# A graph layer on one core: edges over 128 partitions instead of 125, ScalarE with four of the step rows in three groups, and one copy of v moved

## The chip, the cores and the metric

The kernel runs on one core of a Trainium2 chip. The metric is the device time in microseconds (us) of one execution. The program is a single launch.

## The reference

625 nodes with 256 features each, 20,000 edges (`src`, `dst`) sorted by `dst`, and one layer of three parts. What is computed:

```
xn  = layernorm(x)
gnn = (segment_sum(xn[src], dst) / max(count(dst), 1)) @ W_l.T + xn @ W_r.T + b_r
q, k, v = split(xn @ Wqkv.T + bqkv)            # 8 heads of 32
y   = 0.5*(qn.kn)^2 v + sqrt(32)*(qn.kn) v + 32*sum(v), divided by the same with v = 1
x   = x + gnn + y @ Wproj.T + bproj
x   = x + ffn(layernorm(x))                    # GELU, 8 experts, each token takes its best
```

The part that the change touches is the neighbour sum. It isn't gathered row by row: the kernel builds the matrix A (how many edges lead from node s to node t) and multiplies it with `xn @ W_l.T` later.

## The kernel before, in words

**Tiles of nodes.** `TP = 125` nodes make a tile, there are `T = 5` of them, and activations lie as 125 partitions x 5 tiles.

**The matrix A from one-hot products.** The 20,000 edges lie over 125 partitions in 160 chunks (one column of `edges_sb` is a chunk). `GC = 5` chunks make a group, `NG = 32` groups make 16 pairs. For every chunk two rows of 628 half-precision numbers per partition are written into the tensor `oh` (in `mem`): a node row (`node_ids == dst`, always by VectorE, L728) and a step row (whether the column is past `src`). The step rows of a group are shared out by `act_steps(g)`: the first three are ScalarE's (a Sign activation in `step_rows`, L523) and the other two VectorE's (L731). TensorE then accumulates, per chunk, (node row, cut to one tile of 128 columns) times (step row), as two matmuls, L1010 (501 columns) and L1012 (126 columns), in `products(g, tile)`. It accumulates cumulative counts; their differences give A.

**Which tile.** Since edges are sorted by `dst`, a group mostly lies in one tile of nodes. ScalarE, TensorE, VectorE and GpSimd work out in the first 18 us which tile it is and whether there is a second one (`ge`, `edge_tiles`, `flags`). `pair(p)` multiplies two groups for their first tiles, and behind a branch (`other_tiles`) again for a second tile. With the given inputs the five tiles have 3984, 4055, 3973, 4034 and 3954 edges; groups of 625 edges that have two tiles are 6, 12, 19 and 25, which gives (32 + 4) x 5 = 180 calls of the two matmuls.

**Ring of buffers.** `oh` has `OHB = 7` groups; a group g from 7 on may be written when `oh_free` says that group g - 7 (and the pair it is in) was multiplied. VectorE announces a group by `oh_ready`, ScalarE by `steps_ready`; TensorE waits for both before each group.

**Order written out by hand.** All engines have a fixed program. Between the pairs TensorE does 14 small jobs in PSUM bank 7, which are chained by `b7_full` (TensorE to reader) and `b7_free` (reader to TensorE):

- `sums()` (L1044), read by VectorE into `MA` and `ks` (L782, L783). VectorE does groups 3 to 6 before it and 7 and 8 behind it.
- five transposes of q and k (L1051), copied by ScalarE (L598). ScalarE does groups 8 and 9 before the first copy.
- four products U (L1069), read by VectorE into `uq` (L792). VectorE does this before groups 19, 21, 23 and 25.
- four products N (L1074) of `uq`, copied by ScalarE (L606). They stand before pairs (24,25), (26,27), (28,29) and (30,31). Their copies stand on ScalarE behind groups 26, 28, 30 and 31. N number j + 1 waits for `b7_free` of copy j.

When the last pair is done, seven tiny matmuls (L1077) announce `A_done`. ScalarE, VectorE and GpSimd wait for it, then come the differences, attention (L1096, L1117), the projection, the gated network and the experts.

**ScalarE ahead of the pairs** (L549 to L593): the Sign activations of the first groups lie between the copies of the transposed x (`xT_copy`), the squares of q and k (`square`, which wait for VectorE's `biased`), two square roots, and five copies of v and z out of PSUM (`vz_copy`, L572). TensorE clears the banks of A when the copies are made: banks 4, 5, 6 after three copies, bank 0 after four (L999 to L1003), and then starts pair 0. The projection into these banks does not wait for the copies.

Of the kernel before, what the change touches and what calls it, by code (L numbers as in the profile page):

```python
# [6 lines left out]
F16 = mybir.dt.float16  # L7
BF16 = mybir.dt.bfloat16
I32 = mybir.dt.int32
U32 = mybir.dt.uint32  # L10
ALU = mybir.AluOpType
# [3 lines left out]
P = 128  # L15
# [4 lines left out]
def gps_layer(nc, x, edges, w_qkv, b_qk, b_v, w_lr, b_r, w_proj, b_proj, temp,  # L20
              w1, b1, wg, bg, wd, bd, rows_sorted, out):
    N, C = out.shape
    TP = 125
    T = N // TP
    KC = C // P
    NCH = edges.shape[2]
    GC = 5
    NG = NCH // GC
    NP = NG // 2
    OHB = 7  # L30
    OHW = TP * (T - 1) + P
# [14 lines left out]
    assert EB <= T  # L46
    assert N == T * TP and NG * GC == NCH and H == 2 * HG

    with ExitStack() as ctx:
        def sb(name, shape, dt=F32):  # L50
            return ctx.enter_context(nc.sbuf_tensor(name, shape, dt))

        def sem(name):
            return ctx.enter_context(nc.semaphore(name))
# [5 lines left out]
        x_all = sb("x_all", [P, T, C])  # L60
        x_sb = x_all[0:TP]
        edges_sb = sb("edges_sb", [P, 2, NCH], I32)
        src_i, dst_i = edges_sb[0:TP, 0], edges_sb[0:TP, 1]
        wqkv_sb = sb("wqkv_sb", [P, KC, 3 * C])
        bqk_all = sb("bqk_all", [P, 2 * C])
        bqk_sb = bqk_all[0:TP]
# [14 lines left out]
        WD = E * KH * C  # L81
        OH = OHB * 2 * GC * OHW // 2
        BIG = 2 * KH * N
        assert OH + 6 * N <= WD + BIG and T * (N + 1) <= WD
        mem = sb("mem", [P, WD + BIG])
# [1 line left out]
        big = mem[:, WD:WD + BIG]  # L87
        ident = sb("ident", [P, P])
        blk = sb("blk", [P, P])
        node_ids = sb("node_ids", [TP, OHW], F16)  # L90
        ids_m1 = sb("ids_m1", [TP, OHW], F16)
        ones_c = sb("ones_c", [P, P])
        sc2_col = sb("sc2_col", [P, 1])
        root = sb("root", [P, 1])
        base_col = sb("base_col", [P, 1])
        zeros = sb("zeros", [TP, BANK], BF16)
        thr = sb("thr", [TP, T + 1])
        below = sb("below", [TP, T - 1])
        erank = sb("erank", [TP, E])

        src_f = sb("src_f", [TP, NCH])
        dst_f = sb("dst_f", [TP, NCH])
        half_src = sb("half_src", [TP, NCH])
        tile_of = sb("tile_of", [1, T, NG])
        edge_tiles = sb("edge_tiles", [1, 2, T - 1, NG])
        between = sb("between", [1, T, NG])
        span = sb("span", [1, NG])
        two_code = sb("two_code", [1, NG])
        more_code = sb("more_code", [1, NG])
        ones_col = sb("ones_col", [TP, 1], BF16)  # L110
        pair_hi = sb("pair_hi", [1, NP])
        flags = sb("flags", [1, NP], I32)
        more = sb("more", [1, T, NG], I32)
        at_sb = sb("at_sb", [P, T * N])
        QB = P + 1
        qk_sb = sb("qk_sb", [P, T * 4 * QB])
        oh = mem[0:TP, 0:OH].bitcast(BF16).rearrange("p (b w j n) -> p b w j n", b=OHB, w=2, j=GC)
        cum = mem[0:TP, 0:T * (N + 1)].rearrange("p (t n) -> p t n", t=T)
        ge = at_sb[0:TP, 2 * T * C:2 * T * C + (T - 1) * NCH // 2].bitcast(BF16).rearrange("p (k g j) -> p k g j", k=T - 1, j=GC)
        hT = big[:, 0:KH * N].rearrange("p (k n) -> p k n", k=KH)  # L120
        hT_step = big[:, KH * N:KH * N + EB * KH * TP].rearrange("p (b k n) -> p b k n", b=EB, k=KH)

# [41 lines left out]
        PW = N + N % 2  # L164
        lgT = yT_sb[:, 0:N]
        perm = at_sb[0:TP, 0:T * PW // 2].bitcast(BF16).rearrange("p (t n) -> p t n", t=T)
# [18 lines left out]
        pos_f = sb("pos_f", [TP, T])  # L185
# [39 lines left out]
        steps_ready = sem("steps_ready")  # L225
# [34 lines left out]
        flag_read = sem("flag_read")  # L260
# [62 lines left out]
            yield AT[:, 4, TW:N], ps[0:TP, 6, 0:TP]  # L323


        def act_steps(g):
            return 3


        QKV_BANKS = (7, 4, 5, 6, 0, 4, 5, 6, 0, 7)  # L330
# [20 lines left out]
        def x_bank(j):  # L351
            return ps[:, 4 + j, :]
# [162 lines left out]
        def _(act):  # L515
# [5 lines left out]
            def step_rows(g, first, last):  # L521
                for j in range(first, last):
                    ins = nc.scalar.activation(oh[:, g % OHB, 0, j, :], ids_m1[:, :], ACT.Sign,  # L523
                                               bias=half_src[:, g * GC + j:g * GC + j + 1])
                return ins

            def fill(g):
                if g >= OHB:
                    act.wait_ge(oh_free, g - OHB + 1)
                step_rows(g, 0, act_steps(g)).then_inc(steps_ready, 1)  # L530
# [5 lines left out]
            def square(t):  # L536
                act.wait_ge(qk_ready, t + 1)
                nc.scalar.activation(sq[:, t, :].rearrange("p (b c) -> p b c", b=4), qk[:, t, :, 0:P], ACT.Square
                                     ).then_inc(sq_ready, 1)
# [8 lines left out]
            def xT_copy(j):  # L548
                own = slice(2 * TP * j, min(2 * TP * (j + 1), N))  # L549
                act.wait_ge(xT_ps, j + 1)  # L550
                nc.scalar.copy(xnT[:, :, own], x_bank(j)[:, 0:KC * (own.stop - own.start)].rearrange(  # L551
                    "p (c n) -> p c n", c=KC)).then_inc(xT_copied, 1)
# [9 lines left out]
            xT_copy(0)  # L562
            root_part(1)
            step_rows(0, 2, act_steps(0)).then_inc(steps_ready, 1)
            fill(1)
            xT_copy(1)
            square(0)
            xT_copy(2)

            def vz_copy(t):  # L570
                act.wait_ge(qkv_ps, T + t + 1)
                nc.scalar.copy(vz[:, t, 0:2 * C], ps[0:TP, QKV_BANKS[T + t], :]).then_inc(vz_ready, 1)  # L572

            square(1)
            fill(2)
            step_rows(3, 0, 1)
            square(2)
            square(3)
# [4 lines left out]
            nc.scalar.activation(nrm[:, :, 0, :], nrm[:, :, 0, :], ACT.Sqrt, scale=SC2)  # L583
            nc.scalar.activation(nrm[:, :, 1, :], nrm[:, :, 1, :], ACT.Sqrt).then_inc(std_ready, 1)
            step_rows(3, 2, act_steps(3)).then_inc(steps_ready, 1)
            vz_copy(1)
            vz_copy(2)
            fill(4)
            vz_copy(3)
            fill(5)  # L590
            vz_copy(4)
# [23 lines left out]
            for u, (hg, hf, m, pr) in enumerate(units):  # L615
                lo, hi = HALF[hf]
                w = hi - lo
# [3 lines left out]
                b = 2 * (u % SLOTS)  # L621
# [52 lines left out]
        def _(dve):  # L674
# [24 lines left out]
            def normalised(n):  # L699
                lo, hi = LN_PARTS[n]  # L700
                dve.wait_ge(std_ready, n + 1)
                step(nc.vector.reciprocal(rstd[:, lo:hi], rstd[:, lo:hi]))
                for t in range(lo, hi):
                    nc.vector.tensor_scalar(xn[:, t, :], x_sb[:, t, :], mv[:, t, 0:1], rstd[:, t:t + 1],
                                            ALU.subtract, ALU.mult).then_inc(xn_ready, 1)
# [9 lines left out]
            variances(2, T)  # L715
            dve.wait_ge(flag_sum, 1)
            past_first = ps[0:1, 0, 0:(T - 1) * NG].rearrange("p (k g) -> p k g", k=T - 1)
            nc.vector.tensor_scalar(edge_tiles[:, 0], past_first, GC * TP - 1.0, None, ALU.is_gt)
            nc.vector.tensor_scalar(edge_tiles[:, 1], past_first, 1.0 - GC * TP, None, ALU.is_gt).then_inc(flag_read, 1)
            normalised(1)  # L720
            dve.wait_ge(ids_ready, 1)

            def fill(g):
                if g >= OHB:
                    dve.wait_ge(oh_free, g - OHB + 1)
                for j in range(GC):
                    col = g * GC + j
                    ins = nc.vector.tensor_scalar(oh[:, g % OHB, 1, j, :], node_ids[:, :], dst_f[:, col:col + 1], None,  # L728
                                                  ALU.is_equal)
                    if j >= act_steps(g):  # L730
                        ins = nc.vector.tensor_scalar(oh[:, g % OHB, 0, j, :], ids_m1[:, :], src_f[:, col:col + 1], 2.0,  # L731
                                                      ALU.is_ge, ALU.mult)
                ins.then_inc(oh_ready, 1)

            def fill_past(job):
                for g in dve_groups(job):
                    fill(g)
# [6 lines left out]
            def head_sums(t):  # L744
                dve.wait_ge(sq_ready, t + 1)
                return nc.vector.tensor_reduce(nrm[:, t].rearrange("p w h -> p (w h)"),
                                               sq[:, t, :].rearrange("p (h d) -> p h d", d=D), AX.X, ALU.add)

            fill(0)
            dve.wait_ge(in_bqk, 16)  # L750
            biased(0)
            biased(1)
            head_sums(0)
            fill(1)
            biased(2)
            head_sums(1)
# [77 lines left out]
            for t in range(T):  # L834
                a, rest = (ps[0:TP, b, :] for b in RP_BANKS[t % 2])
# [56 lines left out]
            step(nc.vector.tensor_reduce(pos_f[:, :], at_e[:, :, :].rearrange("p e t -> p t e"), AX.X, ALU.add))  # L892
            nc.vector.tensor_copy(pos[:, :], pos_f[:, :]).then_inc(pos_ready, 1)  # L893
            for t in range(T):
                nc.vector.tensor_scalar(perm[:, t, :], node_ids[:, 0:PW], pos_f[:, t:t + 1], None, ALU.is_equal
                                        ).then_inc(perm_ready, 1)

            step(nc.vector.tensor_tensor(past[:, :, :], ahead[0:1, 1:E, 0:1].broadcast_to([1, E - 1, T - 1]),
# [43 lines left out]
        def _(pe):  # L942
# [62 lines left out]

            def products(g, tile):
                buf = g % OHB
                for j in range(GC):
                    node_of = oh[:, buf, 1, j, bass.ds(tile * TP, P)]
                    mm(psf[:, bass.ds(tile * BANK, TW + 1)], node_of, oh[:, buf, 0, j, 0:TW + 1],  # L1010
                       start=False, stop=False, skip_group_check=True)
                    mm(psf[:, bass.ds(tile * P + 5 * BANK, AW)], node_of, oh[:, buf, 0, j, TW:N + 1],  # L1012
                       start=False, stop=False, skip_group_check=True)
# [145 lines left out]
            for t in range(T):  # L1159
# [3 lines left out]
                b, b2 = RP_BANKS[t % 2]  # L1163
# [39 lines left out]
            for part in range(2):  # L1203
                lo, hi = columns(part)
                for k in range(KH):
                    n = KH * part + k
# [72 lines left out]


_OUT = (625, 256)


# [42 lines left out]
```

## Time and profile before

| | us |
|---|---|
| median of 3 runs | 252.06 |
| lowest, highest | 251.73, 252.9 |
| the profiled execution's own time | 251.73 |
| its span, first to last instruction | 250.0 |
| TensorE busy | 235.7 (94%) |
| VectorE busy | 148.2 (59%) |
| ScalarE busy | 145.2 (58%) |
| GpSimd busy | 31.7 (13%) |
| mean granted TensorE clock | 0.997 of full speed |

A busy share is a mean over the span. The one-hot stage lies from about 11 us to 92.6 us; in it VectorE and ScalarE are nearly always busy, and after it much less. What bounds a stretch is read from the chain of work that ended last and from the timelines of the engines beside it.

### The profile page before, as it was taken

How to read it: one execution, taken by the hardware profiler on the slowest of the kernel's cores; microseconds unless marked ns; L12 is line 12 of the kernel's file. 1: busy time of each engine (PE TensorE's matmuls, PEld its weight loads, DVE VectorE, ACT ScalarE, POOL GpSimd, SP SyncE). 2: the span in 40 equal slices, each digit the busy share in tenths (PEclk: the TensorE clock that was granted, in tenths of full speed). 3: DMA queues.
4: the chain of work that ended last, by engine and by line, in shares of the span. 5: the costliest groups of instructions: out<-in, count | busy, mean ns of one | idle time of the engine just before them, and what ended most of it. 6: DMA issues, size and time to landing. Idle time of an engine off the chain costs nothing.

```text
span 250.0 us, 4726 instructions
## 1 busy us (share of the span) xinstructions
PE 235.7 (94%) x1428; PEld 149.4 (60%) x1429; DVE 148.2 (59%) x422; ACT 145.2 (58%) x223; POOL 31.7 (13%) x64
## 2 busy tenths in 40 slices
PE   7899999999897999999999999998899999999990
PEld 2448676655454553433378886564455578888880
DVE  2999999999999969950134649523700243223320
ACT  3977998999999967899950116443043332333000
POOL 7460000000000019100000000000540000000331
PEclk9999999999999999999999999999999999999998
DMA  6560000000000000199910000030123000000111
GB/s 233 194 215 3 1 3 5 3 4 5 0 5 3 3 3 3 37 413 425 416 59 4 0 0 0 24 134 9 32 79 106 0 1 3 0 1 3 38 34 33
DMA packets 6030, 15.82 MB, mean 63 GB/s; under 512 B 2724, under 2 KB 3783, under 8 KB 4723
## 3 DMA queue, kind: packets, MB, share of 16 engines
q1 hardware_dynamic: 4432, 12.64, 13.6%
q0 software_dynamic: 1280, 1.31, 2.0%
q10 hardware_dynamic: 288, 1.44, 1.4%
q8 instruction: 21, 0.34, 0.6%
q14 instruction: 9, 0.07, 0.1%
HBM read 14.08 MB, written 1.30 MB: 62 GB/s over the span
## 4 chain that ended last, share of the span: by engine, by line
PE 69%; DVE 26%; ACT 1%; issue 1%; POOL 1%; DVEq 0%; POOLq 0%
PE ps L1276 17%; DVE mem L728 14%; PE ps L1214 7%; PE ps L1096 7%; PE ps L1260 6%; DVE mem L731 6%; PE ps L1117 5%; PE ps L1176 4%; PE ps L1010 4%; PE ps L1244 3%; PE ps L945 3%; PE ps L1165 2%; PE ps L1167 2%; PE ps L973 1%; DVE qk_sb L774 1%
## 5 line engine op out<-in xcount | busy, mean ns | idle before, releaser
L523 ACT ACTIVATE mem<-ids_m,half_src 125x628 bf16<-125x628 f16 x96 | 69.8, 815 | 0.0
L1010 PE MATMUL ps<-mem 125*128 125x501 bf16 x180 | 51.3, 374 | 2.2 <-issue 2.0
L728 DVE TENSOR_SCALAR mem<-node_ids,dst_f 125x628 bf16<-125x628 f16 x160 | 52.1, 371 | 0.0
L1276 PE MATMUL ps<-mem 128*125 x192 | 41.6, 379 | 0.0
L1012 PE MATMUL ps<-mem 125*128 125x126 bf16 x180 | 39.3, 219 | 0.0
L1276 PEld LDWEIGHTS ps<-mem 128*125 128x125 f32 x192 | 36.0, 188 | 5.4
L1010 PEld LDWEIGHTS ps<-mem 125*128 x180 | 17.6, 98 | 22.5 <-issue 4.8
L622 ACT ACTIVATE qk_sb<-ps,sc_col 125x626 f32<-125x626 f32 (+1 forms) x40 | 28.6, 779 | 3.7 <-PE ps L1096 3.7
L731 DVE TENSOR_SCALAR mem<-ids_m,src_f 125x628 bf16<-125x628 f16 x64 | 23.9, 374 | 0.0
L671 ACT COPY mem<-mem 128x1000 f32 x8 | 8.2, 1031 | 19.8 <-PE ps L1276 19.8
L1096 PE MATMUL ps<-mem 32*125 32x313 f32 (+1 forms) x160 | 19.1, 472 | 0.2 <-DVE mem L801 0.2
L1012 PEld LDWEIGHTS ps<-mem 125*128 x180 | 17.5, 97 | 2.3 <-issue 1.2
L1214 PE MATMUL ps<-xnT,w_sb 128*128 128x375 f32 (+1 forms) x64 | 18.4, 432 | 0.0
L935 DVE SCALAR_TENSOR_TENSOR row<-vz,row x12 | 5.8, 485 | 20.1 <-issue 20.1
L920 DVE COPY mem<-mem 128x500 f32 (+2 forms) x12 | 4.1, 393 | 20.3 <-ACT mem L663 20.0
L505 POOL DMA_INDIRECT rows_sorted<-row,pos x5 | 6.2, 1236 | 77.3 <-DVE pos L893 76.1
L1260 PE MATMUL ps<-xnT,w_sb 128*128 128x512 f32 (+1 forms) x56 | 15.3, 433 | 0.0
L1117 PE MATMUL ps<-qk_sb,vz 125*32 125x313 f32 (+1 forms) x160 | 14.7, 439 | 0.6 <-ACT qk_sb L622 0.6
L1096 PEld LDWEIGHTS ps<-mem 32*125 32x125 f32 x160 | 8.9, 180 | 10.5 <-issue 5.0
L1214 PEld LDWEIGHTS ps<-xnT,w_sb 128*128 128x128 f32 x64 | 11.6, 189 | 5.5 <-ACT mem L651 1.2
L973 PE MATMUL ps<-wqkv_sb,xnT 128*125 128x512 f32 (+1 forms) x40 | 14.1, 487 | 0.8 <-ACT xnT L551 0.8
L651 ACT ACTIVATE mem<-ps,b_sb 128x375 f32<-128x375 f32 (+1 forms) x16 | 8.3, 522 | 9.4 <-PE ps L1214 9.4
(204 smaller groups left out, 280.0 us busy)
## 6 DMA issues: line engine op xcount, KB each, us to landing
mem<-in_wd SPq DMA_DIRECT2D x8, 1024.0 KB, 13.1
w_sb<-in_w SPq DMA_DIRECT2D x1, 1024.0 KB, 8.2
vz<-in_bd SPq DMA_DIRECT2D x1, 1000.0 KB
wqkv_sb<-in_w_qkv ACTq DMA_DIRECT2D x1, 768.0 KB, 6.1
x_all<-in_x ACTq DMA_DIRECT2D x1, 640.0 KB, 4.7
row<-rows_sorted SPq DMA_DIRECT2D x1, 579.7 KB
wlr_sb<-in_w_lr SPq DMA_DIRECT2D x1, 512.0 KB, 5.5
bqk_all<-in_b_qk SPq DMA_DIRECT2D x1, 256.0 KB, 4.7
```

What stands on the lines that cost most here:

```text
L523: ins = nc.scalar.activation(oh[:, g % OHB, 0, j, :], ids_m1[:, :], ACT.Sign, bias=half_src[:, g * GC + j:g * GC + j + 1])
L622: nc.scalar.activation(gsq[:, u % NGB, :, 0:w], ps[0:TP, b:b + 2, 0:w], ACT.Square, bias=sc2_col[0:TP, :]).then_inc(g_ready, 1)
L728: ins = nc.vector.tensor_scalar(oh[:, g % OHB, 1, j, :], node_ids[:, :], dst_f[:, col:col + 1], None, ALU.is_equal)
L731: ins = nc.vector.tensor_scalar(oh[:, g % OHB, 0, j, :], ids_m1[:, :], src_f[:, col:col + 1], 2.0, ALU.is_ge, ALU.mult)
L973: ins = mm(ps[0:TP, QKV_BANKS[n], lo:hi], xnT[:, c, TP * t:TP * (t + 1)], w[:, c, :], start=(c == 0), stop=(c == KC - 1))
L1010: mm(psf[:, bass.ds(tile * BANK, TW + 1)], node_of, oh[:, buf, 0, j, 0:TW + 1], start=False, stop=False, skip_group_check=True)
L1012: mm(psf[:, bass.ds(tile * P + 5 * BANK, AW)], node_of, oh[:, buf, 0, j, TW:N + 1], start=False, stop=False, skip_group_check=True)
L1096: ins = mm(ps[0:TP, 2 * ((2 * u2 + h // 2) % SLOTS) + h % 2, 0:hi - lo], kT[rows, hg, TP * m:TP * (m + 1)], qT[rows, hg, lo:hi], start=Tru ...
L1117: ins = mm(ps[D * h:D * (h + 1), 6 + k % 2, 0:hi - lo], v[:, m, P * hg + D * h:P * hg + D * (h + 1)], gsq[:, (2 * u2 + pr) % NGB, i, 0:hi ...
L1214: ins = mm(fa_bank(part, k), w1_sb[:, c, P * k:P * (k + 1)], x2nT[:, c, lo:hi], start=(c == 0), stop=(c == KC - 1))
L1260: ins = mm(psf[:, at + lo:at + hi], w1_sb[:, c, P * k:P * (k + 1)], x2nT[:, c, lo:hi], start=(c == 0), stop=(c == KC - 1))
L1276: ins = mm(ps[0:TP, 4 + n % EB, 0:C], hT_step[:, n % EB, k, :], wd_sb[:, bass.ds(e, 1), k, :], start=(k == 0), stop=(k == KH - 1))
```

## The change

`edges` is laid out on the host as 160 chunks of 128 edges: 20,000 real edges fill 156 chunks and 32 places of chunk 157; spare places have `src = 0` and `dst = 627`, a column that no tile's output uses. Tensors that were `[TP, ...]` on this path become `[P, ...]` with P = 128 partitions, and the thresholds that tell tiles apart count `GC * P`. Group 31 has two chunks to multiply instead of five (`chunks(g)`). Groups 2, 3 and 9 have four step rows by ScalarE and one by VectorE; of group 31's two, one each. One row of group 2 is written earlier on ScalarE, and `vz_copy(2)` stands behind group 4 instead of ahead of it.

```diff
+    CHUNKS = -(-_EDGES // P)
-        src_i, dst_i = edges_sb[0:TP, 0], edges_sb[0:TP, 1]
+        src_i, dst_i = edges_sb[:, 0], edges_sb[:, 1]
-        node_ids = sb("node_ids", [TP, OHW], F16)
-        ids_m1 = sb("ids_m1", [TP, OHW], F16)
+        node_ids = sb("node_ids", [P, OHW], F16)
+        ids_m1 = sb("ids_m1", [P, OHW], F16)
...
-        oh = mem[0:TP, 0:OH].bitcast(BF16).rearrange(...)
+        oh = mem[:, 0:OH].bitcast(BF16).rearrange(...)
...
+        def chunks(g):
+            return min(GC, CHUNKS - g * GC)
+
         def act_steps(g):
-            return 3
+            if g in (2, 3, 9):
+                return 4
+            return 3 if chunks(g) == GC else chunks(g) // 2
...
             xT_copy(1)
+            step_rows(2, 0, 1)
             square(0)
             xT_copy(2)
...
             square(1)
-            fill(2)
+            step_rows(2, 1, act_steps(2)).then_inc(steps_ready, 1)
             step_rows(3, 0, 1)
...
             step_rows(3, 2, act_steps(3)).then_inc(steps_ready, 1)
             vz_copy(1)
+            fill(4)
             vz_copy(2)
-            fill(4)
             vz_copy(3)
...
-            nc.vector.tensor_scalar(edge_tiles[:, 0], past_first, GC * TP - 1.0, None, ALU.is_gt)
+            nc.vector.tensor_scalar(edge_tiles[:, 0], past_first, GC * P - 1.0, None, ALU.is_gt)
...
@@ fill(g) of VectorE @@
-                for j in range(GC):
+                for j in range(chunks(g)):
@@ products(g, tile) of TensorE @@
-                for j in range(GC):
+                for j in range(chunks(g)):
...
+    def chunked(numbers, fill):
+        spare = np.full(160 * 128 - _EDGES, fill, numbers.dtype)
+        return np.concatenate([numbers, spare]).reshape(160, 128).T
...
-        "edges": partitions(np.stack([a[k].reshape(-1, tp).T for k in ("src", "dst")], axis=1)),
+        "edges": np.ascontiguousarray(np.stack([chunked(a["src"], 0), chunked(a["dst"], 627)], axis=1)),
```

## Rows read from the trace of the kernel before

**Rows 1.** The chain that ended last: start us, us, what held it.

```profile
36.72 0.29 DVE mem L731
37.01 0.20 DVE MA L782
...
75.77 0.46 DVE yT_sb L792
76.27 0.80 PE ps L1074 x2
...
90.96 0.06 issue
91.02 0.37 PE ps L1010
...
92.75 0.69 DVE mem L801
```

**Rows 2.** Busy time by stretch, 28.7 to 92.7 us; us, then busy of PE, PEld, DVE, ACT, POOL.

```profile
28.70:36.90 8.20, 8.20 (x66) 5.78 (x65) 8.20 (x29) 8.20 (x13) 0.00 (x0) 1.00 0.01 3
36.90:39.90 3.00, 3.00 (x25) 1.87 (x23) 3.00 (x14) 2.05 (x4) 0.00 (x0) 1.00 0.02 5
39.90:57.10 17.20, 16.84 (x129) 10.28 (x128) 17.20 (x60) 17.20 (x26) 0.00 (x0) 1.00 0.01 3
57.10:76.20 19.10, 17.17 (x116) 9.54 (x113) 19.10 (x65) 19.10 (x28) 0.00 (x0) 1.00 0.01 3
76.20:92.70 16.50, 15.54 (x110) 8.82 (x111) 14.35 (x50) 14.61 (x23) 0.00 (x0) 1.00 0.01 3
```

**Rows 3.** VectorE in order of time, 28 to 98 us: start, us, instruction.

```profile
28.73 1.25 DVE L728 TENSOR_SCALAR mem<-node_ids,dst_f 125x628 bf16<-125x628 f16 x4
...
30.78 1.25 DVE L728 TENSOR_SCALAR mem<-node_ids,dst_f 125x628 bf16<-125x628 f16 x4
...
36.93 0.28 DVE L782 TENSOR_TENSOR MA<-ps,blk 128x128 f32<-128x128 f32 x1
...
90.18 0.38 DVE L731 TENSOR_SCALAR mem<-ids_m,src_f 125x628 bf16<-125x628 f16 x1
```

**Rows 4.** TensorE in order of time, 24 to 58 us.

```profile
27.88 1.03 PE L945 MATMUL ps<-zeros 125*128 125x512 bf16 x4
28.74 0.38 PE L1010 MATMUL ps<-mem 125*128 125x501 bf16 x1
...
34.20 2.48 PE L1044 MATMUL ps<-qk_sb 125*128 125x129 f32 x20
36.51 0.38 PE L1010 MATMUL ps<-mem 125*128 125x501 bf16 x1
...
39.24 0.62 PE L1051 MATMUL ps<-ident,qk_sb 125*128 125x125 f32 x4
```

**Rows 5.** TensorE in order of time, 88 to 93 us.

```profile
88.83 0.77 PE L1074 MATMUL ps<-yT_sb,blk 128*128 128x312 f32 x2
...
90.53 0.37 PE L1010 MATMUL ps<-mem 125*128 125x501 bf16 x1
...
91.02 0.37 PE L1010 MATMUL ps<-mem 125*128 125x501 bf16 x1
91.29 0.38 PE L1010 MATMUL ps<-mem 125*128 125x501 bf16 x1
...
92.38 0.16 PE L1038 MATMUL ps<-zeros 125*128 125x2 bf16 x1
92.40 0.31 PE L1077 MATMUL ps<-zeros 125*128 125x2 bf16 x7
```

**Rows 6.** ScalarE in order of time, 12 to 41 us; brackets: idle before.

```profile
12.63 0.56 ACT L551 COPY xnT<-ps 128x500 f32<-128x500 f32 x1
14.03 0.63 ACT L538 ACTIVATE at_sb<-qk_sb 125x512 f32<-125x512 f32 x1 [0.84 <-DVE qk_sb L741]
...
24.62 0.59 ACT L572 COPY vz<-ps 125x512 f32<-125x512 f32 x1 [0.54 <-PE ps L973]
25.11 2.24 ACT L523 ACTIVATE mem<-ids_m,half_src 125x628 bf16<-125x628 f16 x3
27.25 0.57 ACT L572 COPY vz<-ps 125x512 f32<-125x512 f32 x1
...
39.90 0.58 ACT L598 COPY mem<-ps 128x500 f32<-128x500 f32 x1 [0.95 <-PE ps L1051]
```

**Rows 7.** ScalarE in order of time, 87 to 92 us.

```profile
87.75 0.52 ACT L606 ACTIVATE mem<-ps,base_col 128x313 f32<-128x313 f32 x1
88.16 2.25 ACT L523 ACTIVATE mem<-ids_m,half_src 125x628 bf16<-125x628 f16 x3
90.28 0.52 ACT L606 ACTIVATE mem<-ps,base_col 128x312 f32<-128x312 f32 x1
```

More of the change, by code:

```diff
@@ L97, in gps_layer @@
         thr = sb("thr", [TP, T + 1])
-        below = sb("below", [TP, T - 1])
+        below = sb("below", [P, T - 1])
         erank = sb("erank", [TP, E])
-        src_f = sb("src_f", [TP, NCH])
-        dst_f = sb("dst_f", [TP, NCH])
-        half_src = sb("half_src", [TP, NCH])
+        src_f = sb("src_f", [P, NCH])
+        dst_f = sb("dst_f", [P, NCH])
+        half_src = sb("half_src", [P, NCH])
         tile_of = sb("tile_of", [1, T, NG])
@@ L109, in gps_layer @@
         more_code = sb("more_code", [1, NG])
-        ones_col = sb("ones_col", [TP, 1], BF16)
+        ones_col = sb("ones_col", [P, 1], BF16)
         pair_hi = sb("pair_hi", [1, NP])
@@ L116, in gps_layer @@
         qk_sb = sb("qk_sb", [P, T * 4 * QB])
-        oh = mem[0:TP, 0:OH].bitcast(BF16).rearrange("p (b w j n) -> p b w j n", b=OHB, w=2, j=GC)
+        oh = mem[:, 0:OH].bitcast(BF16).rearrange("p (b w j n) -> p b w j n", b=OHB, w=2, j=GC)
         cum = mem[0:TP, 0:T * (N + 1)].rearrange("p (t n) -> p t n", t=T)
-        ge = at_sb[0:TP, 2 * T * C:2 * T * C + (T - 1) * NCH // 2].bitcast(BF16).rearrange("p (k g j) -> p k g j", k=T - 1, j=GC)
+        ge = at_sb[:, 2 * T * C:2 * T * C + (T - 1) * NCH // 2].bitcast(BF16).rearrange("p (k g j) -> p k g j", k=T - 1, j=GC)
         hT = big[:, 0:KH * N].rearrange("p (k n) -> p k n", k=KH)
@@ L717, in _ @@
             past_first = ps[0:1, 0, 0:(T - 1) * NG].rearrange("p (k g) -> p k g", k=T - 1)
-            nc.vector.tensor_scalar(edge_tiles[:, 0], past_first, GC * TP - 1.0, None, ALU.is_gt)
-            nc.vector.tensor_scalar(edge_tiles[:, 1], past_first, 1.0 - GC * TP, None, ALU.is_gt).then_inc(flag_read, 1)
+            nc.vector.tensor_scalar(edge_tiles[:, 0], past_first, GC * P - 1.0, None, ALU.is_gt)
+            nc.vector.tensor_scalar(edge_tiles[:, 1], past_first, 1.0 - GC * P, None, ALU.is_gt).then_inc(flag_read, 1)
             normalised(1)
@@ L894, in _ @@
             for t in range(T):
-                nc.vector.tensor_scalar(perm[:, t, :], node_ids[:, 0:PW], pos_f[:, t:t + 1], None, ALU.is_equal
+                nc.vector.tensor_scalar(perm[:, t, :], node_ids[0:TP, 0:PW], pos_f[:, t:t + 1], None, ALU.is_equal
                                         ).then_inc(perm_ready, 1)
@@ L1281 @@
 _OUT = (625, 256)
+_EDGES = 20000
 def kernel(**inputs):
```

## Prediction, on record before the changed kernel ran

> **What bounds the kernel now.** I read the chain of work that ended last first, then the busy times by stretch, and then the timelines of the three engines side by side. The chain stands on VectorE almost without a break from about 28.8 to 76.2 us, then crosses to TensorE (the product N that waits for the last `uq`) and stays there until `A_done` at about 92.7 us [rows 1]. The busy times say the same: VectorE has no gap up to 76.2 us, TensorE has gaps of 1.93 us between 57.1 and 76.2 us, and behind 76.2 us VectorE runs out of work and TensorE sets the end [rows 2]. ScalarE has no gap either from 57.1 to 76.2 us [rows 2]: it is a near second, and the question of this change is whether it becomes the first. After `A_done` everything is released by it, and I let the rest of the kernel move as a block: no transfer or engine behind it has a start of its own that the change moves.
>
> **Prices.** VectorE makes one row (node or step) every 0.293 us: seven rows lie between the starts at 28.73 and 30.78 us, 2.05 us [rows 3]. ScalarE makes one in 0.713 us: three rows lie between the starts at 25.11 and 27.25 us, 2.14 us [rows 6]. TensorE takes 0.27 us for a chunk's two matmuls, the starts at 91.02 and 91.29 us [rows 5].
>
> The page "VectorE: DVE Perf Modes" of the Trainium skill (section "The DRAIN you can't avoid") says that a next operation does not start until the pipe is empty. By it a row would be worth its whole length, 0.37 us, and the one row that counts below would save 0.08 us more. The trace disagrees: four rows that are 1.25 us long together are part of a pace of 0.293 us each [rows 3], so I stay with the pace.
>
> **The change part by part.**
>
> *VectorE before `sums`.* Groups 2 and 3 lose a step row each on VectorE: 2 x 0.293 = 0.59 us. VectorE would reach `MA` (L782) at 36.93 - 0.59 = 36.34 us [rows 3]. But `MA` reads what TensorE's `sums()` writes, and these 20 matmuls end at 34.20 + 2.48 = 36.68 us by their row, or at 36.51 us by the start of the next one [rows 4]. TensorE doesn't get there sooner: from 27.88 us on it works through four bank clears and two pairs without a wait [rows 4]. So a new wait stands at `MA`, and most of the two rows is lost in it. Behind it are VectorE's groups 7 and 8 and all later ones, and for these TensorE. VectorE starts `MA` at about 36.72 us, 0.04 us behind the modelled end, as L801 does behind L1077 (92.75 against 92.40 + 0.31 = 92.71 us) [rows 1, 5]. Gain 0.21 us; bounds 0 (a longer wake-up than this) and 0.42 us (matmul really ends at 36.51 us). I take 0.21, since it goes by the row's own end.
>
> *VectorE, group 9.* One row less behind `MA`: 0.29 us. Bounds 0.29 and 0.37 us, the row's length. VectorE's last `uq`, which releases N 0 at 76.27 us, is then 0.21 + 0.29 = 0.50 us sooner. VectorE has no wait for a free buffer on the way (it never idles [rows 2]), and TensorE, with its 1.93 us of gaps there, can follow.
>
> *ScalarE's three extra rows* cost 3 x 0.713 = 2.14 us if nothing covers them. Group 2's lies between `xT_copy(1)` and `square(0)`, where ScalarE idles 0.84 us for VectorE [rows 6]: 0.71 us fits, cost 0; `square(0)`, `xT_copy(2)` behind it stay where they are. Group 3's pushes `vz_copy(1)` by 0.71 us. Then the moved copy counts: `vz_copy(2)` had waited 0.54 us for its projection [rows 6], and behind group 4 its data are there, so that idle time goes. By starts: `vz_copy(3)` begins at about 27.30 instead of 27.25 us and ScalarE is 0.05 us late (0.17 us at most, 0.71 - 0.54). Group 9's row comes before the first copy of transposed q and k, ahead of which ScalarE idles 0.95 us [rows 6]: 0.95 - 0.17 - 0.71 leaves at least 0.07 us. From the copy at 39.90 us on ScalarE keeps its old times. Cost 0 in all; if the covers were gone, 2.14 us, which is the slower rival.
>
> *The moved copy's other side.* TensorE clears banks 4, 5, 6 after `vz_copy(2)` and bank 0 after `vz_copy(3)`. The former now ends near 27.4 us instead of 25.2, the first clear starts at 27.88 us, and the fourth some 0.6 us later, by when `vz_copy(3)` (27.30 + 0.57 = 27.87 us) is done [rows 4, 6]. Cost 0; bounds 0 and 0.3 us. ScalarE issues no DMA here, and no queue is passed.
>
> *The last group.* VectorE has 3 rows for 7, ScalarE 1 for 3, so group 31 is ready before TensorE is. It had waited: the last chunk of group 30 starts at 90.53, one chunk later would be 90.80, and group 31 starts at 91.02 us [rows 5]. Gain 0.22 us. Three chunks fewer to multiply: 3 x 0.27 = 0.81 us, on the chain. Groups of 640 edges with two tiles are 6, 12, 18 and 25 (the tiles' edge counts end at 3984, 8039, 12012, 16046), again four, so 177 calls instead of 180; 18 and 19 are one pair, so no branch is added.
>
> *ScalarE's guard at N 3.* N 3 (88.83 us) waits for ScalarE's copy of N 2, which ends at 87.75 + 0.52 = 88.27 us and does not move [rows 5, 7]. So what arrives from VectorE is cut off at 88.83 - 88.27 = 0.56 us. The 0.50 us passes.
>
> *128 partitions instead of 125.* The trace has no row of these forms on 128 partitions. Nearest: ScalarE's copies take 0.58 us for 128x500 and 0.57 to 0.59 us for 125x512 [rows 6]. I take 0. The upper bound is 128/125, 2.4% of VectorE's 39.5 us from `MA` to 76.2 us and of TensorE's 16.3 us at the end: 0.95 + 0.39 = 1.3 us. A gain below 0 has no mechanism: no row shrinks.
>
> **Sum.** 0.21 + 0.29 + 0.22 + 0.81 = 1.53 us off `A_done`. The profiled execution took 251.73 us (span 250.0, 1.73 around it): 250.2 us. The median of the runs is 0.33 us above it, so 252.06 - 1.53 = 250.5 us.
>
> **Rivals.**
>
> *Only the tail counts (251.0 us).* The new wait at `MA` eats all of the two rows, or ScalarE is a little late at 39.90 us and its copy holds N 3 at the old time. Then 0.22 + 0.81 = 1.03 us remains. For it: the margins are thin, 0.07 us on ScalarE and 0.06 us at N 3. Against it: each would have to be missed by half a us to take the whole 0.50.
>
> *ScalarE becomes the bound (252.7 us, slower).* Place: N 3's wait for the copy of N 2. If the idle times do not take the three rows, ScalarE is 2.14 us late, the copy ends at 90.41 us, N 3 starts at about 90.47 instead of 88.83 (+1.64), and the tail gives back 1.03: +0.61 us. From 0.56 us of delay it costs, and from 1.59 us on the kernel is slower. For it: ScalarE is without a gap from 57.1 us on. Against it: the idle times of 0.84, 0.54 and 0.95 us stand where the rows are put.
>
> *128 partitions cost (251.8 us).* The upper bound above, 1.3 us, against the gain of 1.53: -0.2 us. For it nothing but the lack of a row; against it the equal copies.
>
> *The change doesn't do what it says.* The chunks do go, and 180 to 177 is sure from the inputs. It could be taken back behind `A_done`; nothing there has a fixed time, so I give it no price of its own and put it with the one above.
>
> **How the numbers follow.** The forecast has 0.69, with its own range 250.1 to 251.0; the tail alone 0.13; ScalarE the bound 0.08; 128 partitions or a gain taken back 0.10. The range for 8 in 10 takes in the tail-only case and nearly the partitions': 249.9 to 251.9 us. Half a per cent, about what a measurement tells from no change, is 1.26 us: below 250.80 us is faster. Of the forecast 0.59 lies below it and 0.10 above; the tail case is all within (0.13); of the rest 0.12 is within and 0.06 slower. Faster 0.59, same 0.35, slower 0.06.
>
> **What would show it.** Right: VectorE idle for up to 0.4 us before L782 with PE L1044 named, and the last `uq` near 75.2 us; ScalarE's gaps before L538 (0.84) and L598 (0.95) gone or under 0.2 us, the copy of N 2 still near 87.75 us; N 3 near 88.3 us; no wait before group 31; 177 calls of L1010; L801 near 91.2 us; rows on VectorE still 0.293 us apart. Wrong: N 3 waiting for ScalarE's L606, pair 0 later than 28.74 us, a wait on TensorE before a group for ScalarE's rows, or a distance between L801 and the end that differs from before's.

## The result, and the profile after

The changed kernel takes 250.26 us (median of 6 runs, 250.15 to 250.71) against 252.09 us before (6 runs, 251.68 to 252.9). The ratio is 0.9929, 95% interval 0.9914 to 0.9944. Forecast were 250.5 us, with 249.9 to 251.9 as the range. The profiled executions differ by less: 251.73 to 250.31 us, spans 250.0 to 248.6 us, 1.4 us. One of the six runs of e5_group9 took 344.03 us at a granted clock of 0.659 and is left out as a slow run; every other run here is a fast one.

Where the 1.4 us are is seen at three places of the timelines. First VectorE of the changed kernel, 20 to 98 us (start, us, instruction, in brackets the idle time before it), to be held against [rows 3]:

```profile
36.09 0.38 DVE L738 TENSOR_SCALAR mem<-ids_m,src_f 128x628 bf16<-128x628 f16 x1
36.84 0.29 DVE L789 TENSOR_TENSOR MA<-ps,blk 128x128 f32<-128x128 f32 x1 [0.37 <-PE ps L1051]
...
75.32 0.53 DVE L799 SCALAR_TENSOR_TENSOR yT_sb<-ps,ks,mem 128x312 f32<-128x312 f32 x1
...
91.34 2.63 DVE L808 COPY mem<-ps 125x501 f32<-125x501 f32 x5 [2.32 <-PE ps L1084]
```

The wait that the forecast put ahead of `MA` is there, 0.37 us, and names the matmuls of `sums` (now L1051). `MA` starts only 0.09 us sooner than before, although VectorE had two rows less to do. The last `uq` starts 0.37 us sooner (75.69 before), the copies behind `A_done` 1.41 us sooner. Then TensorE, as in [rows 4] and [rows 5]:

```profile
27.93 1.03 PE L952 MATMUL ps<-zeros 125*128 125x512 bf16 x4
...
34.33 2.48 PE L1051 MATMUL ps<-qk_sb 125*128 125x129 f32 x20
...
88.46 0.78 PE L1081 MATMUL ps<-yT_sb,blk 128*128 128x312 f32 x2
...
90.16 0.37 PE L1017 MATMUL ps<-mem 128*128 128x501 bf16 x1
90.42 0.37 PE L1017 MATMUL ps<-mem 128*128 128x501 bf16 x1
90.69 0.38 PE L1017 MATMUL ps<-mem 128*128 128x501 bf16 x1
90.97 0.17 PE L1045 MATMUL ps<-zeros 125*128 125x2 bf16 x1
90.99 0.31 PE L1084 MATMUL ps<-zeros 125*128 125x2 bf16 x7
```

Pair 0 starts at 28.79 us (before 28.74), later by just as much as the clears (27.93 against 27.88), so this is the stage's start, and not the sign against the forecast that a pair 0 held up by the moved copy would have been. N 3 starts at 88.46 instead of 88.83 us (0.37). Of the three L1017 rows at the end the first is the last chunk of group 30; group 31 follows it without a gap and has two chunks. From N 3 to L1084 it is 2.53 us, before it was 3.57: 1.04 us. And ScalarE, as in [rows 6] and [rows 7]:

```profile
13.14 0.82 ACT L529 ACTIVATE mem<-ids_m,half_src 128x628 bf16<-128x628 f16 x1
14.08 0.63 ACT L544 ACTIVATE at_sb<-qk_sb 125x512 f32<-125x512 f32 x1
...
24.27 0.56 ACT L579 COPY vz<-ps 125x512 f32<-125x512 f32 x1
24.73 2.24 ACT L529 ACTIVATE mem<-ids_m,half_src 128x628 bf16<-128x628 f16 x3
26.87 1.05 ACT L579 COPY vz<-ps 125x512 f32<-125x512 f32 x2
...
40.03 0.58 ACT L605 COPY mem<-ps 128x500 f32<-128x500 f32 x1 [0.28 <-PE ps L1058]
...
87.88 0.52 ACT L613 ACTIVATE mem<-ps,base_col 128x313 f32<-128x313 f32 x1
88.28 0.82 ACT L529 ACTIVATE mem<-ids_m,half_src 128x628 bf16<-128x628 f16 x1
89.28 0.52 ACT L613 ACTIVATE mem<-ps,base_col 128x312 f32<-128x312 f32 x1 [0.17 <-PE ps L1081]
```

Group 2's early row fills the idle 0.84 us ahead of the square, and of the 0.95 us ahead of the first copy of q and k 0.28 us are left. The copy of N 2 starts at 87.88 us against 87.75 before. It ends at 88.40, and N 3 starts at 88.46: there is nothing to spare there now.

The page of the changed kernel (part 5: instructions and their mean ns) has these rows on 128 partitions:

```profile
L529 ACT ACTIVATE mem<-ids_m,half_src 128x628 bf16<-128x628 f16 x97 | 70.6, 813 | 0.0
L1017 PE MATMUL ps<-mem 128*128 128x501 bf16 x177 | 50.2, 374 | 1.7 <-issue 1.5
L735 DVE TENSOR_SCALAR mem<-node_ids,dst_f 128x628 bf16<-128x628 f16 x157 | 51.6, 383 | 0.0
```

There are 177 calls for 180. ScalarE's mean is 813 ns (815 before), TensorE's 374 as before. VectorE's says 383 instead of 371 ns, but its rows still start 0.293 us apart: from the `uq` at 66.23 us to the next at 70.78 us lie 14 rows and one `uq` in 4.55 us, and before it was 66.59 to 71.14, 4.55 us too. The mean of one instruction is not its price when instructions overlap. Nor do the runs show that the 12 ns come from the partitions: by the pages of the experiments below, the same row on 128 partitions is 371 ns long in e7_uncovered and 398 ns in e9_ma_late.

### The profile page after: what moved, and what is told of

Its sections match the earlier page's. It is cut to its first block, busy times and chain, and to the rows that moved or that the text cites. A ratio compares the mean times of both kernels' runs of the same rounds, so it can differ in the third digit from the quotient of the medians.

```text
span 248.6 us, 4705 instructions
## 1 busy us (share of the span) xinstructions
PE 234.3 (94%) x1422; PEld 148.8 (60%) x1423; DVE 146.3 (59%) x415; ACT 145.8 (59%) x224; POOL 31.8 (13%) x64
## 4 chain that ended last, share of the span: by engine, by line
PE 75%; DVE 18%; DMA 2%; ACT 1%; issue 1%; POOL 0%; DVEq 0%; ACTq 0%
PE ps L1283 17%; DVE mem L735 11%; PE ps L1221 7%; PE ps L1103 7%; PE ps L980 7%; PE ps L1267 6%; PE ps L1017 5%; PE ps L1124 5%; PE ps L1183 4%; DVE mem L738 4%; PE ps L1251 3%; PE ps L1172 2%; PE ps L1174 2%; DMA edges_sb<-in_edges 2%; PE ps L1019 1%
## 5 line engine op out<-in xcount | busy, mean ns | idle before, releaser
L529 ACT ACTIVATE mem<-ids_m,half_src 128x628 bf16<-128x628 f16 x97 | 70.6, 813 | 0.0
L1017 PE MATMUL ps<-mem 128*128 128x501 bf16 x177 | 50.2, 374 | 1.7 <-issue 1.5
L735 DVE TENSOR_SCALAR mem<-node_ids,dst_f 128x628 bf16<-128x628 f16 x157 | 51.6, 383 | 0.0
L1019 PE MATMUL ps<-mem 128*128 128x126 bf16 x177 | 38.7, 219 | 0.0
L1017 PEld LDWEIGHTS ps<-mem 128*128 x177 | 17.3, 98 | 21.6 <-issue 3.9
L738 DVE TENSOR_SCALAR mem<-ids_m,src_f 128x628 bf16<-128x628 f16 x60 | 23.1, 386 | 0.0
L1019 PEld LDWEIGHTS ps<-mem 128*128 x177 | 17.2, 97 | 1.9 <-issue 0.7
```

## How the experiments are read

The stage starts up to 0.6 us sooner or later from one profiled execution to the next (27.68 us in e7, 28.30 us in e1); MA, N 3 and the rest move with it. So places are given as distances, in us, from the start of the four bank clears (27.88 in the kernel before, row L945 x4). S is the start of VectorE's copies behind `A_done`, and "rest" is the span, which is given to 0.1 us, less S. All are differences of starts in the timelines of one profiled execution each. The times are medians. Each of the three sets of kernels had its own runs of the kernel before beside it: 252.06 us for e1, e2, e3, e7, 251.95 for e4, e5, e6, e8 and 252.01 for e9, e10, e11. The three sets ran on different chips, so times of different sets are compared by their ratios.

| kernel | MA | last uq | N 3 | S | rest | time | ratio to before, interval |
|---|---|---|---|---|---|---|---|
| before | 9.05 | 47.81 | 60.95 | 64.87 | 157.25 | 252.06 | |
| changed | 8.91 | 47.39 | 60.53 | 63.41 | 157.26 | 250.26 | 0.9929 [0.9914, 0.9944] |
| e1_tail | 8.93 | 47.71 | 60.86 | 63.74 | 157.16 | 251.16 | 0.9961 [0.9948, 0.9974] |
| e2_rows | 8.94 | 47.43 | 60.57 | 64.93 | 157.18 | 252.05 | 1.0006 [0.9989, 1.0024] |
| e3_all160 | 8.95 | 47.42 | 60.60 | 64.93 | 157.24 | 251.75 | 0.999 [0.9981, 0.9998] |
| e4_group2 | 8.84 | 47.32 | 60.47 | 63.35 | 157.13 | 250.55 | 0.994 [0.9928, 0.9953] |
| e5_group9 | 8.91 | 47.69 | 60.83 | 63.71 | 157.22 | 250.56 | 0.9946 [0.9933, 0.9959] |
| e6_copy | 8.87 | 47.33 | 60.50 | 63.38 | 157.23 | 250.47 | 0.9941 [0.9928, 0.9953] |
| e7_uncovered | 9.21 | 47.10 | 62.58 | 65.48 | 157.14 | 252.55 | 1.0019 [1.0011, 1.0028] |
| e8_ma | 10.56 | 46.97 | 60.57 | 63.47 | 157.19 | 250.33 | 0.9935 [0.9922, 0.9948] |
| e9_ma_late | 10.45 | 46.87 | 60.05 | 62.93 | 157.21 | 249.71 | 0.9897 [0.9871, 0.9923] |
| e10_best | 10.52 | 46.64 | 59.95 | 62.83 | 157.19 | 249.63 | 0.9892 [0.9866, 0.9919] |
| e11_after_again | 8.93 | 47.39 | 60.55 | 63.45 | 157.22 | 250.18 | 0.9916 [0.9889, 0.9942] |

Two things are read at once. The rest is the same in all of them, 157.13 to 157.26 us: what is won at S arrives in full. And the changed kernel twice (its row and the last) agrees within 0.04 us at every place.

The places are not always that exact. VectorE has the same work ahead of `MA` in the kernel before, in e1 and in e7, and there `MA` stands at 9.05, 8.93 and 9.21: where VectorE doesn't wait for TensorE, its start against the clears varies by up to 0.28 us. A difference of 0.1 us in such a place is no effect of an edit by itself.

## The experiments: which part brings what

**e1_tail**, partitions and the short last group alone:

```diff
         def act_steps(g):
-            if g in (2, 3, 9):
-                return 4
             return 3 if chunks(g) == GC else chunks(g) // 2
...
-            step_rows(2, 0, 1)
...
-            step_rows(2, 1, act_steps(2)).then_inc(steps_ready, 1)
+            fill(2)
...
             vz_copy(1)
-            fill(4)
             vz_copy(2)
+            fill(4)
```

> 128 partitions and 157 chunks, but ScalarE keeps three step rows in every full group and the old order of its copies. Theory (two gains: 1.03 us at the last group, the rest from VectorE's rows): N 3 stays at 88.8 us, no wait before group 31, the sum copies after A_done start at 91.7 us, 1.03 us sooner than before; time 251.05 us. Rival (only the short last group and its partitions matter, rows on ScalarE bring nothing): the same place as the changed kernel, 91.34 us, time 250.3 us. Rival (128 partitions cost up to 2.4%): N 3 up to 1 us later, rows more than 0.293 us apart.

Measured: S is 1.13 us sooner than before and 0.33 later than in the changed kernel, the time is 251.16 us. N 3 stands where it stood (60.86 against 60.95), within the scatter of `MA`. The theory holds; the rival (rows on ScalarE bring nothing) falls, by place and by time.

**e2_rows**, the rows and the copy alone, on 125 partitions and 160 chunks:

```diff
         def act_steps(g):
-            return 3
+            return 4 if g in (2, 3, 9) else 3
```

and the two edits to ScalarE's order as in the change.

> 125 partitions and 160 chunks as before, but ScalarE has four step rows in groups 2, 3 and 9, one of group 2's early, and the copy of v moved. Theory with a guard behind the last group's rows: N 3 comes at 88.46 us, 0.37 us sooner, but ScalarE's three rows of group 31 end at 90.5 us as before and TensorE starts group 31 at 91.0 us: A_done as before within 0.15 us, time 252.0 us. Rival (the gains add up): sum copies start at 92.38 us, time 251.7 us. Rival (the rows are not covered): N 3 later than 88.8 us.

Measured: N 3 is 0.38 us sooner, S is 0.06 us later than before, the time 252.05 us and the same as before. So the gain of the rows vanishes between N 3 and S. TensorE of e2, 86 to 94 us:

```profile
88.46 0.78 PE L1075 MATMUL ps<-yT_sb,blk 128*128 128x312 f32 x2
91.09 0.37 PE L1011 MATMUL ps<-mem 125*128 125x501 bf16 x1 [0.50 <-issue]
92.47 0.31 PE L1078 MATMUL ps<-zeros 125*128 125x2 bf16 x7
```

and ScalarE of e2:

```profile
88.27 2.25 ACT L523 ACTIVATE mem<-ids_m,half_src 125x628 bf16<-125x628 f16 x3
```

TensorE stands idle before group 31 until 91.09 us. VectorE's last row of it ended at 89.82 + 0.37 = 90.19 us, ScalarE's third at 88.27 + 2.25 = 90.52. ScalarE holds a second guard there, three rows of group 31, and they don't get sooner when VectorE does. The trace puts the idle time down to "issue"; that it is ScalarE is read from the two ends: TensorE starts 0.57 us behind ScalarE's, as it does in e3 (90.75 to 91.32 us), and 0.90 us behind VectorE's. This guard could be seen before the change: there ScalarE's third row ended at 88.16 + 2.25 = 90.41 us [rows 7], and by an estimate with the same 0.57 us it would have let group 31 start at 90.98, only 0.04 us ahead of where it did.

**e3_all160**, the changed kernel with the spare chunks written and multiplied:

```diff
         def chunks(g):
-            return min(GC, CHUNKS - g * GC)
+            return GC
```

> The changed kernel with all 160 chunks of 128 written and multiplied, the last three of spare edges only. Theory: N 3 at 88.46 us as changed; ScalarE's three rows of group 31 end at about 90.5 us, TensorE starts group 31 at 91.0 us, sum copies at 92.7 us: 1.35 us slower than the changed kernel and equal to before within 0.15 us. Rival (only the three chunks count, 0.81 us): 92.15 us, time 251.1 us. Rival (partitions cost): slower than before, with rows over 0.293 us apart.

Measured: N 3 is as in the changed kernel, S is 1.52 us later than there and 0.06 later than before, the same numbers as e2. Its time is 251.75 us, 0.1% under before, and the interval just excludes 1; the places give no reason for it. e3 differs from e2 by 128 against 125 partitions, and in what runs only by the second tile of group 18 instead of 19, in the same pair. All places from MA to S agree within 0.03 us, so 128 partitions cost nothing here and gain nothing. The three chunks are worth more than their 0.81 us, because the wait before group 31 goes with them.

**e7_uncovered**, the same three rows of ScalarE where it has no idle time:

```diff
-            if g in (2, 3, 9):
+            if g in (12, 14, 16):
                 return 4
```

and ScalarE's order is as before.

> The changed kernel with ScalarE's three extra step rows in groups 12, 14 and 16 instead of 2, 3 and 9, and the order of its rows and copies as before: no idle time of ScalarE takes them. Theory (the rival ScalarE becomes the bound, put into practice): ScalarE's copy of N 2 ends near 90.4 us, N 3 starts at 90.5 us, 2.0 us later than in the changed kernel, sum copies at 93.4 us, time 0.6 us over before: 252.7 us. Rival (ScalarE has slack, its rows are free wherever they stand): VectorE is 0.88 us ahead and the time is 250.0 us or less.

Measured: VectorE is ahead as the rival wants (last `uq` 47.10), but N 3 comes 1.63 us later than before, S 0.61 us later, time 252.55 us, slower than before by the interval. TensorE of e7 shows the last of the waits:

```profile
90.26 0.79 PE L1080 MATMUL ps<-yT_sb,blk 128*128 128x312 f32 x2 [0.49 <-ACT mem L612]
```

N 3 starts 0.05 us behind the end of ScalarE's copy of N 2 (89.69 + 0.52 = 90.21 us). The bracket holds only 0.49 us, because TensorE has waited for ScalarE's rows before: group 25, for one, starts 0.57 us behind ScalarE's last row of it and 1.57 us behind VectorE's. This is the rival "ScalarE becomes the bound" with its price: forecast were +1.64 at N 3 and +0.61 in all. What separates the changed kernel from it is that its rows lie in idle time.

## The experiments: where the rows' gain goes

**e4_group2** and **e5_group9**, one of the three rows given back:

```diff
-            if g in (2, 3, 9):
+            if g in (3, 9):            (e4)
+            if g in (2, 3):            (e5)
```

> The changed kernel with three step rows of group 2 by ScalarE instead of four: VectorE has one row more before MA. Theory (a new wait at MA swallows it): VectorE's idle time before MA falls from 0.37 to 0.08 us, MA still starts at 36.84 us, time as changed (250.3 us, sum copies at 91.34 us). Rival (each row off VectorE counts): 0.29 us slower, sum copies at 91.63 us.

> The changed kernel with three step rows of group 9 by ScalarE. Theory: this row is behind MA, so the last uq and N 0 come 0.29 us later, the sum copies at 91.63 us, time 250.55 us; ScalarE's idle time before its first copy of q and k grows from 0.28 to about 1.0 us. Rival (ScalarE's copy of N 2 is what holds N 3): nothing changes, 91.34 us.

Measured: e4's S stands at 63.35, 0.06 us sooner than in the changed kernel. Of the idle time ahead of `MA` 0.10 us is left:

```profile
36.56 0.40 DVE L738 TENSOR_SCALAR mem<-ids_m,src_f 128x628 bf16<-128x628 f16 x1
37.06 0.29 DVE L789 TENSOR_TENSOR MA<-ps,blk 128x128 f32<-128x128 f32 x1
```

`MA` starts 2.51 us behind the start of `sums` in both (6.33 to 8.84, and 6.40 to 8.91 in the changed kernel). Group 2's row is worth nothing, as the wait at `MA` swallows it. e5's S stands at 63.71, 0.30 us later, and ScalarE idles 0.98 us before its first copy: group 9's row is worth its 0.29 us. The times don't settle this. The medians of the two are equal (250.55 and 250.56 us), and e4's alone would fit its rival, 0.29 us slower than the 250.26 us of the changed kernel, which wasn't run in this set; the ratios' intervals overlap. It is the places that tell them apart.

**e6_copy**, the moved copy put back:

```diff
             vz_copy(1)
-            fill(4)
             vz_copy(2)
+            fill(4)
```

> The changed kernel with vz_copy(2) back ahead of group 4. Theory (ScalarE has 0.28 us to spare at 39.75 us and nothing to spare at N 3): the wait of 0.5 us for the projection comes back, ScalarE's first copy of q and k starts about 0.26 us later, its copy of N 2 ends at 88.66 us and N 3 starts at 88.7 us, sum copies at 91.6 us, 0.26 us slower than changed. Rival (the move does nothing): 91.34 us.

Measured: S is at 63.38, no difference by place, and the expected 0.26 us did not come. (The median, 250.47 us, can't decide it, for the same reason as in e4.) ScalarE of e6, 22.6 to 31 us:

```profile
22.84 1.51 ACT L529 ACTIVATE mem<-ids_m,half_src 128x628 bf16<-128x628 f16 x2
24.25 1.05 ACT L579 COPY vz<-ps 125x512 f32<-125x512 f32 x2
25.20 2.24 ACT L529 ACTIVATE mem<-ids_m,half_src 128x628 bf16<-128x628 f16 x3
```

The two copies follow each other without a wait. In the kernel before `vz_copy(2)` waited until 24.62 us. Group 3's fourth row puts everything behind it 0.71 us later, so the projection is there by the time of the copy. The idle 0.54 us was taken by the row itself, and I had given that to the move. The move of the copy does nothing that this trace shows.

**e8_ma** and **e9_ma_late**: VectorE's group 7 goes ahead of `MA`, so that the wait has work in it; e9 also gives one step row of group 28, behind the last `uq`, back to VectorE.

```diff
+            fill(DVE_AHEAD)
             dve.wait_ge(b7_full, JOB_M + 1)
...
             ins.then_inc(b7_free, 1)
-            fill_past(JOB_M)
+            fill(DVE_AHEAD + 1)
...
+            if g in (28,):             (e9 only)
+                return 2
```

> The changed kernel with VectorE's group 7 put ahead of MA, so that it has no wait there. Theory with ScalarE's guard at N 3: VectorE gains 0.37 us and the last uq ends near 75.4 us, N 0 starts at 75.5 us, but N 3 waits for ScalarE's copy of N 2 and stays at 88.46 us, sum copies at 91.34 us, time as changed. Rival (VectorE alone sets it): N 3 at 88.1 us, sum copies at 90.97 us, 0.37 us faster.

> The changed kernel with VectorE's group 7 ahead of MA (no wait there), and one step row of group 28 given back from ScalarE to VectorE, which takes 0.71 us off ScalarE ahead of its copy of N 2. Theory (VectorE up to its last uq, and ScalarE's copy of N 2 as the guard, each must move): the last uq ends near 75.4 us, the copy of N 2 near 87.7 us, N 3 starts at 88.1 us without a wait, sum copies 0.37 us sooner than in the changed kernel, time 249.9 us. Rival (TensorE itself is the limit between 57 and 76 us): no gain over the changed kernel.

Measured: in e8 the last `uq` is 0.42 us sooner than in the changed kernel (46.97), N 3 is not (60.57). TensorE of e8:

```profile
88.51 0.79 PE L1082 MATMUL ps<-yT_sb,blk 128*128 128x312 f32 x2 [0.29 <-ACT mem L613]
```

That is ScalarE's guard at N 3: its copy of N 2 ends at 87.93 + 0.53 = 88.46 us, 0.05 us ahead. In e9 ScalarE makes its copy of N 2 at 87.02 us, TensorE doesn't wait there, and N 3 is at 60.05, S at 62.93: 0.48 us sooner than the changed kernel, 249.71 us. Forecast were 0.37. The 0.11 us above it are in VectorE's start: with the same work ahead of `MA` as in e8, `MA` stands at 10.45 against 10.56. The edit doesn't account for that; it is of the size of the scatter named above. By time, the gain over e11, which ran in the same set, is 0.47 us.

**e10_best** is e9 with one row more by ScalarE before the last `uq` (group 12), and one more by VectorE behind it (group 27). Against the changed kernel, besides the two edits at `MA`:

```diff
-            if g in (2, 3, 9):
+            if g in (2, 3, 9, 12):
                 return 4
+            if g in (27, 28):
+                return 2
```

> The kernel of e9 with a fourth step row by ScalarE in group 12, and one row each of groups 27 and 28 given back to VectorE. Theory: VectorE's group 25 is ready 0.66 us sooner than in the changed kernel, ScalarE's 0.71 us later and now level with it (near 77.3 us), so that TensorE starts group 25 about 0.55 us sooner and everything behind follows: time 249.75 us. Rival (ScalarE's group 25 is late and takes the gain back): no better than e9, 249.9 us, with a wait on TensorE for ScalarE's rows before group 25.

Measured: S at 62.83, 0.58 us sooner than the changed kernel (forecast 0.55), time 249.63 us; by its places 0.10 us sooner than e9, by its time not to be told from it. Its median is the lowest that was run. VectorE and ScalarE of e10 are now level at group 25:

```profile
74.60 5.07 ACT L531 ACTIVATE mem<-ids_m,half_src 128x628 bf16<-128x628 f16 x7
...
77.13 0.39 DVE L740 TENSOR_SCALAR mem<-ids_m,src_f 128x628 bf16<-128x628 f16 x1
...
78.11 0.37 PE L1020 MATMUL ps<-mem 128*128 128x501 bf16 x1 [0.44 <-issue]
```

VectorE's last row of the group ends at 77.52 us. ScalarE's is the fourth of the seven shown (one is of group 24, then three of group 25), and at 0.713 us a row it ends near 77.5 us as well. TensorE starts the group at 78.11 us.

**e11_after_again** is the changed kernel once more:

> The changed kernel once more, unchanged, to stand beside e9 and e10 on the same chip: 250.3 us, N 3 60.5 us behind the clearing of the banks.

Measured 250.18 us, N 3 at 60.55.

## Why the prediction was right, point by point

- *The bound.* VectorE up to the last `uq`, then TensorE: right. The gain at the last `uq` is the gain at N 3 in the changed kernel and in e1, e2, e3, e4, e5, e6 and e9 (N 3 less last `uq` is 13.14 to 13.18 us in all of them and before). In e7 and e8 it isn't, where ScalarE holds N 3; in e10 N 0 follows the last `uq` as elsewhere (0.61 us), but the pair behind it, with group 25, takes 0.13 us longer than in e9, and the difference is 13.31 us. The crossing lies one group later than the forecast had it. Before, VectorE's last row of group 25 ends at 78.27 us, and TensorE, through with group 24, starts group 25 only at 78.78, which the trace calls "issue":

```profile
77.90 0.37 DVE L731 TENSOR_SCALAR mem<-ids_m,src_f 125x628 bf16<-125x628 f16 x1
...
78.78 0.37 PE L1010 MATMUL ps<-mem 125*128 125x501 bf16 x1 [0.36 <-issue]
```

The last `uq` and group 25 came sooner by the same 0.37 us in the changed kernel (group 25: 78.78 to 78.41), so it made no difference to the sum.

- *The wait at MA, 0.21 us forecast, 0.09 measured.* The mechanism is right (0.37 us idle, and e4). The size is short by 0.12 us: the stage began 0.05 us later in this execution (27.93 against 27.88), and `sums` began another 0.08 us later (6.40 against 6.32 us behind the clears). The latter is seen in e2, e3, e5, e8 and e11 as well and not in e1, e4, e6, e7, e9 and e10; in the changed kernel TensorE has a gap of 0.07 us before group 2 (31.49 to 31.58 us, before 31.45 to 31.47). Up to that place e9 and e10 run the same program as e8, so the edits don't decide it. What makes it is open. With `sums` at 6.33 (e4) `MA` is 0.21 us sooner than before, the forecast's number, though before's 9.05 has the scatter of VectorE's start in it.
- *Group 9's row, 0.29 us:* e5 shows 0.30.
- *The last group, 0.22 + 0.81 = 1.03 us:* 1.04 measured from N 3 to L1084, and e1.
- *ScalarE's rows for nothing:* right in the sum, with one wrong reason. The move of `vz_copy(2)` was credited with the idle time that group 3's row takes up by itself (e6).
- *The guard at N 3:* right and shown by e8. But its margin was put too wide. When N 3 waits for the copy it starts 0.05 us behind the copy's end (e7, e8), so what can pass is about 0.5 us and not 0.56; in the changed kernel it starts 0.06 us behind it, and VectorE and ScalarE arrive there together. And I saw it as the only guard. The three rows of group 31 on ScalarE are another (e2, e3), and it is the short last group that opens it. So the terms were not independent, as the sum had them: the rows alone give -0.06, the short group alone 1.13, both 1.46 us at S. The sum came out right because both parts were in the change; this dependence it had not reckoned with, and in that it was lucky.
- *128 partitions for nothing:* right, by e3 against e2.
- *Nothing given back behind `A_done`:* right, 157.13 to 157.26 us in all kernels.

Sum: 1.53 us forecast, 1.41 at S, 1.4 in the spans. The medians differ by 1.83 us; the interval of the ratio, times 252.09, is 1.41 to 2.17 us. The remaining 0.4 us between the medians and the profile has to do with which executions were profiled: that of before was the second shortest of its six, 0.36 us under their median, and that of the changed kernel the fourth shortest, 0.05 us over it. Whether a mechanism is behind it as well is open. Against it stands that single runs of before spread over 1.2 us; for it, that e11 beside its own runs of before gives 1.83 us again (252.01 to 250.18). No trace shows where it would be.

The page "VectorE: DVE Perf Modes" of the Trainium skill (section "The DRAIN you can't avoid") says that the next operation waits for an empty pipe, and the prediction stopped there; the section also says that a next operation that is not held starts earlier. The changed trace agrees with this second sentence: its rows are 0.38 us long and start 0.293 us apart.

## What to carry to other kernels

Work moved to an engine that is nearly always busy is free only in what idle time it has: held against e1 at S, the same three rows won 0.33 us in groups 2, 3 and 9 and lost 1.74 us in groups 12, 14 and 16 (e7). So look for the idle time upstream of the point at which other engines wait for it, and check each such point behind it: here ScalarE guarded N 3 by a copy and group 31 by three rows. Test a gain one wait further down: the rows' 0.38 us at N 3 was nothing at the end until another edit took the next wait away. And where an engine catches up into a new wait, as at `MA`, give it its next piece of work before the wait: that, with one row handed back behind the last `uq`, was worth 0.48 us at S, where all three rows together were worth 0.33.

## What the runs showed of the hardware

The recorded length of a VectorE row differs from execution to execution and is not its price. Node rows on 128 partitions are 371 ns (e7) to 398 ns (e9) long by mean, on 125 partitions 371 and 372 ns (before, e2), and their starts stay 0.293 us apart.

When TensorE has to wait for the second group of a pair, its first matmul starts 0.46 to 0.51 us after the end of VectorE's last row, where that is what it waits for (before, group 31: 90.56 to 91.02 us; group 25: 78.27 to 78.78 us), and 0.57 us after the end of ScalarE's (e2, group 31: 90.52 to 91.09 us; e3: 90.75 to 91.32 us). The trace calls that idle time "issue". So a group that is ready only just in time still makes TensorE wait: before, group 31's last row ended 0.24 us ahead of 90.80 us, when TensorE could have gone on, and it went on 0.22 us late.
